# Moving expert 0's first low parts to GpSimd, and reordering the list and step-word work ahead of the expert steps

## The reference

```python
x = x + depool(layernorm(x) through rmsnorm and W_in, rmsnorm(context), lengths)
z = layernorm(x)                                    # 2048 tokens of 256
probs = softmax(z @ gate_w); top 2 of 8 experts, weights renormalised
for i in range(8):
    h = silu(z @ w1[i]) * (z @ w3[i])               # 256 -> 1024
    out += (h @ w2[i]) * weight_i
x = x + out
```

## Time and profile before

| | us |
|---|---|
| median of 3 timed runs | 452.12 |
| the profiled execution | 447.69 |
| its span, first to last instruction | 445.7 |
| TensorE busy | 402.4 (90%) |
| VectorE busy | 303.7 (68%) |
| GpSimd busy | 243.7 (55%) |
| mean granted TensorE clock | 0.982 |

### The profile page before, as it was taken

One profiled execution on the slowest core, in us unless ns is written; L12 is line 12 of the kernel. 1 busy time (PEld: TensorE's weight loads), 2 busy tenths in 40 slices (PEclk: granted clock), 3 DMA queues, 4 the chain that ended last, 5 costly groups with the idle time before them and its releaser, 6 DMA issues.

```text
span 445.7 us, 12041 instructions
## 1 busy us (share of the span) xinstructions
PE 402.4 (90%) x2300; PEld 335.6 (75%) x2304; DVE 303.7 (68%) x820; ACT 193.8 (43%) x335; POOL 243.7 (55%) x251
## 2 busy tenths in 40 slices
PE   0669999879899999999999999999999999799963
PEld 0557776336688888888888888888888888688862
DVE  7997689886764776556857665766876457755540
ACT  2574347014623463336435623563554336443320
POOL 6428556024574676447755883676576535435342
PEclk9999988899999999999999999999999999999989
DMA  6954996605976787658877896798788554535542
GB/s 190 353 175 146 335 339 197 228 26 151 302 237 166 203 271 233 172 150 243 262 213 222 231 253 170 220 252 242 220 258 255 161 146 140 162 99 153 140 116 25
DMA packets 80361, 89.81 MB, mean 202 GB/s; under 512 B 8071, under 2 KB 60583, under 8 KB 80343
## 3 DMA queue, kind: packets, MB, share of 16 engines
q1 hardware_dynamic: 64327, 55.24, 38.0%
q0 software_dynamic: 16016, 34.37, 30.9%
HBM read 58.77 MB, written 30.82 MB: 201 GB/s over the span
## 4 chain that ended last, share of the span: by engine, by line
PE 68%; DVE 4%; issue 3%; DVEq 1%; ACT 1%; DMA 1%; POOL 1%; POOLq 0%; ACTq 0%
PE bank L1558 66%; PE bank L1565 2%; DVE split L1323 1%; DMA out<-yblk,itok 1%; ACT split L342 1%; DVE split L348 1%; DVEq L296 0%; DVE hmul L1267 0%; DVE onehot_lo L1180 0%; POOL out L547 0%; DVE hT L1283 0%; PE bank L1581 0%; DVE swap_in L1275 0%; DVEq L348 0%; DVEq L329 0%
## 5 line engine op out<-in xcount | busy, mean ns | idle before, releaser
L1558 PE MATMUL bank<-split,xT_hi 128*128 x592 | 167.7, 404 | 7.0 <-DVE split L348 3.3
L1558 PEld LDWEIGHTS bank<-split,xT_hi 128*128 128x128 f32 x592 | 106.1, 188 | 30.7 <-issue 9.9
L1558 PEld LDWEIGHTS bank<-split,hT 128*128 128x128 f32 x888 | 112.5, 192 | 5.6 <-issue 1.6
L1558 PE MATMUL bank<-split,hT 128*128 (+1 forms) x888 | 114.0, 285 | 1.5 <-ACT yblk L725 0.7
L718 ACT ACTIVATE gact<-bank 128x512 f32<-128x512 f32 x74 | 44.2, 598 | 143.5 <-PE bank L1558 143.5
L1267 DVE TENSOR_TENSOR hmul<-gact,bank 128x512 f32<-128x512 f32 x74 | 50.8, 687 | 76.2 <-ACT gact L718 75.7
L1558 PE MATMUL bank<-split,xT_lo 128*128 x296 | 92.9, 395 | 0.0
L547 POOL DMA_INDIRECT out<-yblk,itok x37 | 72.1, 1947 | 37.0 <-issue 30.5
L530 POOL DMA_INDIRECT xblk<-z_rows,gidx x40 | 41.0, 1024 | 88.4 <-DVE gidx L1306 68.6
L348 DVE TENSOR_TENSOR split<-raw,split x22 | 50.4, 2293 | 27.7 <-ACT split L342 26.9
L1558 PEld LDWEIGHTS bank<-split,xT_lo 128*128 128x128 f32 x296 | 55.6, 188 | 13.4
(11 more groups left out here) (196 smaller groups left out, 339.0 us busy)
## 6 DMA issues: line engine op xcount, KB each, us to landing
raw<-in_L_ffn_w POOLq DMA_DIRECT2D x84, 256.0 KB
swap_rows<-swap_in SPq DMA_DIRECT2D x74, 256.0 KB, 3.3
swap_out<-swap_rows SPq DMA_DIRECT2D x74, 256.0 KB, 3.5
ctx_sb<-in_ctx SPq DMA_DIRECT2D x4, 1024.0 KB, 6.3
raw<-in_L_ffn_w SPq DMA_DIRECT2D x12, 256.0 KB, 6.5
x_all<-in_x SPq DMA_DIRECT2D x4, 512.0 KB, 8.3
depool_rows<-gact SPq DMA_DIRECT2D x4, 512.0 KB, 4.1
out<-x_all SPq DMA_DIRECT2D x4, 512.0 KB, 6.6
```

The costliest lines, as they stand in the source:

```text
L1558: mm = pe.matmul(out_, xp, w_, start=start and n == 0, stop=stop and n == 2)
```

## The change

- `first_up` leaves DVE for GpSimd: it does both halves right behind its loads of expert 1, ahead of the gathers.
- `z_rows` holds a row of zeros at 0 and the tokens' rows at 1 to 2048, so that the numbers of the lists are rows of z as they stand. The index of the gathers is taken from `number`, and the first two columns come straight from the lists. `idx_all`, still needed for adding to `out`, is made later, in `row_places`, which also has what `weight_places` did.
- The number of blocks and the first four field instructions stand ahead of DVE's wait for the lists, and `unused` and `idx_all` no longer stand ahead of the other fields.
- Block 0's transposes on TensorE and its `xT_hi` on ACT come ahead of the wait for the table.
- POOL's `settle`, a semaphore increment ahead of the gather, is left out for blocks 0, 1 and 2 and for others whose number is a constant.

```diff
--- before.py
+++ after.py
@@ -74,7 +74,7 @@
         def sem(name):
             return stack.enter_context(nc.semaphore(name))
 
-        z_dram = nc.dram_tensor("z_rows", (T + P, D), f32, kind="Internal").ap()
+        z_dram = nc.dram_tensor("z_rows", (T + 1, D), f32, kind="Internal").ap()
         w_dram = nc.dram_tensor("w_rows", (2 * T, 1), f32, kind="Internal").ap()
         swap_dram = nc.dram_tensor("swap_rows", (2, 2, P, HALF), f32, kind="Internal").ap()
         depool_dram = [nc.dram_tensor(f"depool_rows{b}", (S, D), f32, kind="Internal").ap() for b in range(B)]
@@ -380,7 +380,7 @@
             load_x(2)
             load_x(3)
             sp.wait_ge(s["pad_ready"], 1)
-            sp.dma_start(z_dram[T:T + P, :], zeros[:, :]).then_inc(s["z_rows"], 16)
+            sp.dma_start(z_dram[0:1, :], zeros[0:1, :]).then_inc(s["z_rows"], 16)
 
 
             def next_ctx(b):
@@ -399,7 +399,7 @@
 
             def z_rows_out(b):
                 sp.wait_ge(s["z_ready"], TPB * (b + 1))
-                sp.dma_start(z_dram[b * S:(b + 1) * S, :].rearrange("(j p) d -> p j d", p=P), z[:, b % 2])\
+                sp.dma_start(z_dram[1 + b * S:1 + (b + 1) * S, :].rearrange("(j p) d -> p j d", p=P), z[:, b % 2])\
                   .then_inc(z_out[b], 16)
 
             def first_weights(m):
@@ -523,10 +523,22 @@
 
 
             raw_load(pool, 1, 1, s["raw_ready"])
+            def first_up(part):
+
+                cols = slice(part * HALF, (part + 1) * HALF)
+                pool.wait_ge(s["hi_ready"], 2)
+                pool.tensor_tensor(up_lo[:, 0, :, :, cols], raw_up[:, 0, :, :, cols],
+                                  up_hi[:, 0, :, :, cols].bitcast(f32), ALU.subtract)\
+                   .then_inc(s["lo_first"], 1)
+
+            first_up(0)
+            first_up(1)
+
             def block_rows(i, q):
 
                 pool.wait_ge(s["gidx_ready"], i + 1)
-                settle(pool)
+                if not isinstance(i, int):
+                    settle(pool)
                 pool.indirect_dma_start(xblk[:, q, :], None, z_dram[:, :],
                                         bass.IndirectOffsetOnAxis(ap=gidx[:, q:q + 1], axis=0))\
                     .then_inc(blk_in[q], 16)
@@ -690,14 +702,15 @@
             act.wait_ge(s["wturn_mm"], 1)
             act.activation(w_turned[:, :], p_wT, ACT.Copy).then_inc(s["wturn_ready"], 1)
 
+            def xT(i, q):
+                act.wait_ge(s["xT_done"], i + 1)
+                act.activation(xT_hi[:, q], p_xT, ACT.Copy).then_inc(s["xThi_ready"], 1)
+
+            xT(0, 0)
             act.wait_ge(s["table_ready"], 1)
             act.wait_ge(s["x1_rows"], 16 * B)
             for b in range(B):
                 act.wait_ge(z_out[b], 16)
-
-            def xT(i, q):
-                act.wait_ge(s["xT_done"], i + 1)
-                act.activation(xT_hi[:, q], p_xT, ACT.Copy).then_inc(s["xThi_ready"], 1)
 
             def hT(q, half, part):
 
@@ -758,7 +771,6 @@
 
             act.sem_inc(s["y_ready"], 2)
             less_two = blocks_less_two(act)
-            xT(0, 0)
             over_steps(act, step)
             at_end(act, less_two, drain)
 
@@ -1182,21 +1194,6 @@
                    .then_inc(s["hi_step"], 1)
 
 
-            dve.wait_ge(s["list_mm"], 1)
-            dve.tensor_copy(second_choice[:, :], p_idx)\
-               .then_inc(s["idx_step"], 1)
-            dve.wait_ge(s["idx_step"], 1)
-            dve.scalar_tensor_tensor(number[:, :], p_idx, -1.0, second_choice[:, :], ALU.mult, ALU.max)\
-               .then_inc(s["idx_step"], 1)
-            dve.wait_ge(s["idx_step"], 2)
-            dve.scalar_tensor_tensor(unused[:, :], number[:, :], 0.0, ids_f[:, B * TPB:B * TPB + 1]
-                                     .broadcast_to([P, TABLE]), ALU.is_equal, ALU.mult).then_inc(s["idx_step"], 1)
-            dve.wait_ge(s["idx_step"], 3)
-            dve.scalar_tensor_tensor(idx_all[:, :], number[:, :], -1.0, unused[:, :], ALU.add, ALU.add)\
-               .then_inc(s["idx_ready"], 1)
-            dve.wait_ge(s["idx_ready"], 1)
-            dve.tensor_copy(gidx[:, :], idx_all[:, 0:2]).then_inc(s["gidx_ready"], 2)
-
             dve.tensor_scalar(blocks_i[:, :], cum[0:1, E - 1:E], -2.0, None, ALU.add).then_inc(s["blocks_ready"], 1)
 
             at = ids_f[:, 0:1]
@@ -1207,6 +1204,16 @@
                .then_inc(s["fields_ready"], 1)
             dve.tensor_scalar(done_before, cum[:, :], -2.0, at, ALU.subtract, ALU.is_lt)\
                .then_inc(s["fields_ready"], 1)
+
+            dve.wait_ge(s["list_mm"], 1)
+            dve.tensor_copy(second_choice[:, :], p_idx)\
+               .then_inc(s["idx_step"], 1)
+            dve.wait_ge(s["idx_step"], 1)
+            dve.scalar_tensor_tensor(gidx[:, :], p_idx[:, 0:2], -1.0, second_choice[:, 0:2], ALU.mult, ALU.max)\
+               .then_inc(s["gidx_ready"], 2)
+            dve.scalar_tensor_tensor(number[:, :], p_idx, -1.0, second_choice[:, :], ALU.mult, ALU.max)\
+               .then_inc(s["idx_step"], 1)
+
             dve.wait_ge(s["fields_ready"], 4)
             dve.tensor_reduce(steps[:, :], stepm[:, :, :], AX.X, ALU.add).then_inc(s["fields_ready"], 1)
             dve.wait_ge(s["fields_ready"], 5)
@@ -1247,12 +1254,20 @@
             dve.wait_ge(s["word_mm"], 1)
             dve.tensor_copy(table[:, :], p_word).then_inc(s["table_ready"], 1)
 
-            def weight_places():
-
-                dve.tensor_scalar(number[:, :], number[:, :], 1.0, -1.0, ALU.max, ALU.add).then_inc(s["idx_step"], 1)
-                dve.tensor_scalar(second_choice[:, :], second_choice[:, :], 0.0, float(T), ALU.is_lt, ALU.mult)                   .then_inc(s["idx_step"], 1)
+            def row_places():
+
+                dve.wait_ge(s["idx_step"], 2)
+                dve.scalar_tensor_tensor(unused[:, :], number[:, :], 0.0, ids_f[:, B * TPB:B * TPB + 1]
+                                         .broadcast_to([P, TABLE]), ALU.is_equal, ALU.mult).then_inc(s["idx_step"], 1)
+                dve.tensor_scalar(second_choice[:, :], second_choice[:, :], 0.0, float(T), ALU.is_lt, ALU.mult)\
+                   .then_inc(s["idx_step"], 1)
+                dve.wait_ge(s["idx_step"], 4)
+                dve.scalar_tensor_tensor(idx_all[:, :], number[:, :], -1.0, unused[:, :], ALU.add, ALU.add)\
+                   .then_inc(s["idx_ready"], 1)
+                dve.wait_ge(s["idx_ready"], 1)
+                dve.tensor_scalar(unused[:, :], number[:, :], 1.0, -1.0, ALU.max, ALU.add).then_inc(s["idx_step"], 1)
                 dve.wait_ge(s["idx_step"], 5)
-                dve.tensor_tensor(widx_all[:, :], number[:, :], second_choice[:, :], ALU.add)\
+                dve.tensor_tensor(widx_all[:, :], unused[:, :], second_choice[:, :], ALU.add)\
                    .then_inc(s["idx_step"], 1)
 
             def xT(i, q):
@@ -1303,7 +1318,7 @@
             def next_index(i, q, half):
 
                 dve.wait_ge(blk_in[q], 16 * half)
-                dve.tensor_copy(gidx[:, q:q + 1], idx_all[:, ds(i, 1)]).then_inc(s["gidx_ready"], 1)
+                dve.tensor_copy(gidx[:, q:q + 1], number[:, ds(i, 1)]).then_inc(s["gidx_ready"], 1)
 
             def weight_index(i, q, half):
 
@@ -1315,14 +1330,6 @@
 
                 dve.wait_ge(s["added_rows"], OUT_INIT + 16 * (i - 1))
                 dve.tensor_copy(itok[:, q:q + 1], idx_all[:, ds(i, 1)]).then_inc(s["meta_ready"], 1)
-
-            def first_up(part):
-
-                cols = slice(part * HALF, (part + 1) * HALF)
-                dve.wait_ge(s["hi_ready"], 2)
-                dve.tensor_tensor(up_lo[:, 0, :, :, cols], raw_up[:, 0, :, :, cols],
-                                  up_hi[:, 0, :, :, cols].bitcast(f32), ALU.subtract)\
-                   .then_inc(s["lo_first"], 1)
 
             def step(i, q, half, word):
                 if not after(i, 1):
@@ -1356,11 +1363,9 @@
             dve.wait_ge(s["x1_rows"], 16 * B)
             for b in range(B):
                 dve.wait_ge(z_out[b], 16)
-            first_up(0)
             xT(0, 0)
             next_index(2, 0, 1)
-            first_up(1)
-            weight_places()
+            row_places()
             dve.wait_ge(s["idx_step"], 6)
             def drain(i, q):
                 perm_last(i, 0)
@@ -1624,9 +1629,9 @@
                 down(i, q, E - 1, (E - 1) & 1, (s["drainlo_ready"], s["drainlo_ready"]), (1, 2))
 
             pe.sem_inc(s["y_done"], 1)
+            xT(0, 0, 0)
             pe.wait_ge(s["table_ready"], 1)
             less_two = blocks_less_two(pe)
-            xT(0, 0, 0)
             keep_clock(4)
             over_steps(pe, step)
             at_end(pe, less_two, drain)
```

## The result

The changed kernel took 458.98 us (median of 5, 458.14 to 462.03), the kernel before 452.12 (median of 5, 449.31 to 454.29); the ratio is 1.0167, 95% interval 1.0128 to 1.0206, which is 7.5 us (5.8 to 9.3). It is slower, where the forecast put it (458.1).

A forecast was written before the change was run, and what follows sets the result against it. VectorE's path ahead of step 0 was taken to bound the start: 8.1 us of stall, less 0.6 absorbed, plus 0.5 slow clock, less 2.0 gained, gives +6.0 on the 452.12 median: 458.1 us, range 449.7 to 460.5.

The forecast's parts named there:

- The mechanism: From 78.3 us, VectorE instructions wait for whole GpSimd subtractions; 4.1 us each costs VectorE almost all of their time.
- Duration of a subtraction: Each GpSimd subtraction of 128x2048 behind the weight loads takes 4.1 us, bounds 2.03 and 6.5.
- The stall: VectorE's second one-hot row, from 78.66, is held until 86.8 by GpSimd's two subtractions: 8.1 us late.
- One DVE instruction between: One VectorE instruction passes between GpSimd's first subtraction, ending at 82.45, and its second, ending at 86.7.
- The absorbed wait: Of VectorE's 1.02 us wait at 82.69 for the rank matmul, some 0.6 us goes, leaving 7.5 us late.
- The slow clock: TensorE idles during VectorE's delay, its clock falls, and twenty fillers ahead of the lists cost 0.5 us more.
- The hand-over: Between the lists and step 0, earlier words, gather, transposes and xT_lo gain 2.0 us, bounds 1.6 to 2.35.
- The sum: VectorE's delay, less absorbed wait, plus slow clock, less the 2.0 us gained behind the lists: +6.0 us, 458.1 us.
- A: Rival: GpSimd and VectorE pass each other, leaving only the 2.0 us gain, 450.1 us; chance 0.28.
- B: Rival: VectorE is held, but GpSimd's subtractions take about 2.03 us each; +1.4 us, 453.5 us; chance 0.12.
- C: Rival: VectorE wins the port, GpSimd's pair stretches past 91.5 and delays the gather; +2.9, 455.0 us at 9 each; chance 0.05.
- D: Rival: TensorE's fillers and register loads hold step 0 near 98.4, so the time is 452 us; chance 0.03.

The follow-up runs named there:

- e2: The kernel before with only expert 0's low-part subtraction moved to GpSimd, behind its loads; ratio 1.0219 to the kernel before, 9.9 us slower.
- e4: The changed kernel with GpSimd's work in eight subtractions of 128x512, each waiting for the one before; ratio 1.0171 to the kernel before, 7.7 us slower.
- e5: The changed kernel with an 8-column GpSimd memset and a wait for it between weight loads and subtractions; ratio 1.0141 to the kernel before, 6.3 us slower.
- e3: The changed kernel with no subtraction, expert 0's low parts being zeros written by GpSimd near 23 us; ratio 1.0023 to the kernel before.
- e6: The changed kernel with no subtraction, expert 0's low parts being zeros written by ScalarE; ratio 0.9943 to the kernel before, 2.6 us faster.

## Why the prediction was right

*The mechanism.* Right, and for the reason given: a VectorE instruction of the kind in question waits for the whole GpSimd instruction. The two rows it was read from, at 9.35 and 94.16, showed 0.2 us of it; the held rows of e2, e4 and e5 end within 0.1 us of GpSimd's. Whether the one-hot rows themselves would stop was left open there, though the sum took them as held; they stopped. Whether `gap`, with two inputs, would have been held too is not shown, as it stood behind them. The Trainium skill, "SBUF — State Buffer", section "Who interferes with whom", states it as a port pair held for a whole instruction; the runs agree on the wait at 11 us, and e3 also for a memset; they cannot show the port.

*Duration of a subtraction.* 4.1 taken, 4.56 measured. The Trainium skill's 4497 ns ("GPSIMD Engine Reference", section 3) was the better value: the rows of one-input instructions, doubled, came out 10% short.

*The stall.* Predicted 8.1 us late, 11.0 measured (11.29 for a row of 0.31). Two steps failed. "One DVE instruction between" the two did not happen: the first and second subtraction left no gap. That cost little. And I started the stall at the subtraction's row, while it starts beside the last loads, 2.2 us earlier (e5). The Trainium skill, "GPSIMD Engine Reference", section 2.1 "Instruction dispatch", says that a core of GpSimd starts the next instruction as soon as its own share of the last is done; that would explain it, if the loads do not occupy all cores. It would also close the gap: cores ahead by 2.2 us would be in the second subtraction while others still did the first, and behind the fence, where all would start together, there is a gap. The fence and the early held row of e4 fit this, but no row here shows single cores, so that much is argued and not shown.

*The absorbed wait.* 0.6 predicted; the wait at `posf` went from 1.02 to 0.47.

*The slow clock.* The clock did fall as forecast: the granted clock was 0.51 from 96 to 100 us, and the twenty fillers took 6.24 us against 4.48. But the predicted 0.5 us was 0: from the fourth `posf` to the copy it is 7.46 us here and 7.47 before. The fillers ended 1.8 us late, and of the slack ahead of the lists I had counted 1.4 us; TensorE's idle times there were 0.99, 0.38 and 0.21 us in the kernel before (at 87.97, 88.76 and 89.55), 1.58 in all. Where the last 0.2 us went is not shown.

*The hand-over.* 2.0 predicted, 2.5 measured; its bound was 2.35. The reduce of the fields came 0.49 us behind the copy (0.59 worked out), the fillers did bind the word (1.47 us of wait gone), and the gather landed in 2.8 us again. Two things were better than counted. Block 0's transposes came 4.17 us behind the copy, with the gather, and not 4.49, and the register load and fillers behind them added nothing to xT_lo: step 0's first matmul is 0.26 us behind the end of xT_lo, where I had put 0.6 us.

*The sum.* +10.3 and -2.5 where +8.0 and -2.0 stood: +7.8 against +6.0. The stall was undersized by 2.9 us: 2.2 for its earlier start and 0.9 for two subtractions of 4.56 in place of 4.1, less 0.2 of rounding and of where the row began. The clock that cost nothing (0.5) and the better hand-over (0.5) took back 1.0. So the forecast was 1.8 us low by the trace's sum, 1.5 by the timed ratio and 0.9 by the medians. That it came out so near is in part luck: the stall alone was 2.9 us too small.

*The rivals.* A did not happen, but e6 shows its world at 2.6 us faster. B fell with the subtractions of 4.56 us. C fell too: GpSimd's pair was not stretched, was done at 90.00, and GpSimd then sat idle for 15.21 us. D fell with step 0 at 5.79 us behind the copy. The chances given for "slower" add up to 0.63, not 0.62.

## What to carry to other kernels

Work given to GpSimd is not free for VectorE because it is on another engine: look at what VectorE does in the same microseconds, and price the move at the whole length of each GpSimd instruction, reads or writes, unless VectorE's instructions there come through. Here one-hot rows of 16-bit and a cast were held and MAX8 was not. A row that is long for its shape and ends with another engine's row is a wait; search for such rows before reading busy shares. And when the work that covered other latencies goes away, follow the next engine's own queue ("issue"): there 1.8 us lay (step 1 at 13.87 against 12.07 us behind the copy) that the reordering of matmuls alone did not reach.

## What the runs showed of the hardware that I had not expected

- A subtraction queued on GpSimd behind DMA issues holds VectorE about 2.2 us before its own row begins (78.77 against 80.98; gone with a fence).
- GpSimd's memsets of 128x2048 (1.77 us each) hold VectorE's one-hot rows like subtractions do: 3.3 us for two.
- Two subtractions back to back leave no gap for a waiting VectorE instruction (one row of 11.29 us), though behind a fence they did (4.71 and 4.29 us). What makes the difference is argued above and not shown. MAX8 passed beside a subtraction (87.71, 0.36 us for four).
- The first 75 us of the same code vary by up to 4 us between executions, and the difference arises between 30 and 40 us: the granted clock of TensorE there was 0.66 in the slowest, 0.83 in those between and 1.00 in the fastest, with sixteen matmuls in 6.7, 5.41 and 3.72 us.
